# Deformable convolution: nine tap shifts of a pair shared 5 to 4 between SyncE and GpSimd, instead of 4 to 5, late in the second layer

## The reference

```python
off1 = make_offset(conv3x3(x, tm1_w, tm1_b), conv3x3(x, tr1_w, tr1_b))
out = deform_conv(x, off1, dcn1_w)
out = relu(batchnorm(out, bn1_g, bn1_b))
off2 = make_offset(conv3x3(out, tm2_w, tm2_b), conv3x3(out, tr2_w, tr2_b))
out = batchnorm(deform_conv(out, off2, dcn2_w), bn2_g, bn2_b)
return relu(out + residual)
```

## Time and profile before

| what | value |
|---|---|
| median of three runs | 427.45 us (426.53 to 428.62) |
| the profiled execution | 429.34 us, of which the span of the trace is 427.5 us |
| TensorE busy | 398.2 us, 93% of the span |
| ScalarE busy | 327.0 us, 76% |
| VectorE busy | 312.3 us, 73% |
| GpSimd busy | 111.4 us, 26% |
| mean granted clock of TensorE | 0.991 |
| `moved<-conv_sb` DMAs | 112 from SyncE, 140 from GpSimd |
| second layer | from about 220 us to 415 us of the span |

### The profile page before, as it was taken

How to read it: one execution, slowest core, us unless ns; L and a number is a source line. 1 busy time by engine, 2 the same in 40 slices (tenths; PEclk the granted TensorE clock), 3 DMA queues, 4 the chain that set the end, 5 groups by cost and what they waited for, 6 DMA issues and landing times.

```text
span 427.5 us, 19117 instructions
## 1 busy us (share of the span) xinstructions
PE 398.2 (93%) x7747; PEld 357.9 (84%) x7747; DVE 312.3 (73%) x868; ACT 327.0 (76%) x423; POOL 111.4 (26%) x241
## 2 busy tenths in 40 slices
PE   4978899999999999999998899999999998999980
PEld 4865689999999999999885788999999997998870
DVE  3649877788887777777438888877777776777445
ACT  2617788888888898888835878888888887888745
POOL 6303223222222222238001322232222222220000
PEclk9999999999999999999999999999999999999996
DMA  6301342211122222222001231222222222222005
GB/s 220 84 2 34 71 69 48 45 36 36 38 46 46 44 44 46 49 48 41 2 3 28 57 62 38 50 45 46 45 45 45 48 48 47 48 48 40 3 2 196
DMA packets 61529, 21.28 MB, mean 50 GB/s; under 512 B 53798, under 2 KB 61308, under 8 KB 61484
## 3 DMA queue, kind: packets, MB, share of 16 engines
q1 hardware_dynamic: 56588, 18.20, 20.3%
q0 software_dynamic: 4896, 2.43, 2.2%
HBM read 3.23 MB, written 2.10 MB: 12 GB/s over the span
## 4 chain that ended last, share of the span: by engine, by line
PE 85%; DVE 5%; DMA 4%; ACT 2%; issue 2%; SPq 1%; POOL 1%; DVEq 0%; ACTq 0%; POOLq 0%
PE acc_ps L746 54%; PE z_ps L719 12%; PE build_ps L704 8%; PE side_ps L652 3%; PE acc_ps L770 3%; PE side_ps L641 2%; DMA xs<-in_x 2%; PE build_ps L588 1%; DMA moved<-conv_sb 1%; PE acc_ps L598 1%; DMA feat_rows<-feats 1%; ACT raw L563 1%; PE acc_ps L630 1%; SPq L278 1%; ACT S L482 0%
## 5 line engine op out<-in xcount | busy, mean ns | idle before, releaser
L746 PE MATMUL acc_ps<-S,Z 64*64 64x256 f32 x4416 | 279.4, 377 | 1.6 <-issue 0.9
L746 PEld LDWEIGHTS acc_ps<-S,Z 64*64 64x64 f32 x4416 | 225.3, 133 | 19.8 <-issue 3.5
L482 ACT ACTIVATE S<-build_ps,minus 128x1024 f32<-128x1024 f32 x190 | 201.5, 1112 | 30.6 <-PE build_ps L704 30.2
L719 PE MATMUL z_ps<-wz,xflat 64*64 64x192 f32 x1536 | 106.9, 328 | 0.0
L704 PE MATMUL build_ps<-feat_rows,cst 64*64 64x512 f16 x576 | 82.9, 377 | 3.3 <-ACT S L482 1.6
L475 ACT ACTIVATE Z<-z_ps 128x768 f32<-128x768 f32 x96 | 78.2, 814 | 4.9 <-PE z_ps L719 4.9
L719 PEld LDWEIGHTS z_ps<-wz,xflat 64*64 64x64 f32 x1536 | 75.8, 132 | 6.5 <-issue 1.3
L1007 DVE TENSOR_SCALAR S<-build_ps 128x512 f32<-128x512 f32 x96 | 66.1, 688 | 19.1 <-PE build_ps L704 17.3
L278 POOL DMA_DIRECT2D moved<-conv_sb x140 | 71.0, 514 | 20.6 <-POOL conv_sb L371 15.5
L1009 DVE TENSOR_SCALAR S<-build_ps 128x512 f32<-128x512 f32 x96 | 65.3, 680 | 0.0
L371 POOL TENSOR_TENSOR conv_sb<-conv_sb,cst 128x32 f32<-128x32 f32 x28 | 7.5, 269 | 200.5 <-ACT conv_sb L469 200.5
(11 more groups left out here) (116 smaller groups left out, 307.4 us busy)
## 6 DMA issues: line engine op xcount, KB each, us to landing
xs<-in_x SPq DMA_DIRECT2D x4, 512.0 KB, 7.5
out<-raw SPq DMA_DIRECT2D x7, 256.0 KB, 2.5
moved<-conv_sb POOLq DMA_DIRECT2D x56, 11.2 KB
moved<-conv_sb SPq DMA_DIRECT2D x56, 11.2 KB
moved<-conv_sb POOLq DMA_DIRECT2D x56, 11.3 KB
wz<-in_dcn_w POOLq DMA_DIRECT2D x2, 288.0 KB, 4.7
feat_rows<-feats SPq DMA_TRANSPOSE x32, 3.7
moved<-conv_sb SPq DMA_DIRECT2D x28, 12.0 KB
```

What stands on the lines that cost most here:

```text
L482: act.activation(S[:, (parity + b) % 2, half, 0:ACT_TAPS, :], build_ps[:, 0:ACT_TAPS, :], ACT.Relu, bias=minus2[:, :], scale=1.0 if half = ...
L719: mm = pe.matmul(z_ps[halves[c], i, h * BLOCK_COLS:(h + 1) * BLOCK_COLS], xflat[parity][halves[i], pixels], wz[halves[i], layer, h, b * BL ...
L746: mm = pe.matmul(acc_ps[halves[i], g, 0:HW], Z[halves[g], slot, i, half, j * C:(j + 1) * C], S[halves[g], slot, half, j, :].rearrange(by_i ...
```

## The change

For the layer with index 1, and from pair 20 on (the third shift of that layer; pairs 18 and 19 come first), SyncE issues the taps 4, 1, 7, 3, 8 and GpSimd 0, 2, 5, 6. Tap 8 moves from the end of GpSimd's list to the end of SyncE's. The values waited for follow from a new helper. Twelve shifts are concerned (pairs 20 to 31).

```diff
+LATE_SP_TAPS, LATE_POOL_TAPS = SP_TAPS + POOL_TAPS[4:], POOL_TAPS[:4]
+EARLY_PAIRS = 4
...
+        def is_late(T, layer):
+
+            return layer == 1 and not (isinstance(T, int) and T - PAIRS < EARLY_PAIRS)
+
+        def shifts(T, layer, taps, late_taps):
+
+            if not is_late(T, layer):
+                return 16 * len(taps) * by_taps(T, layer)
+            early = by_taps(PAIRS * layer + EARLY_PAIRS - 1, layer)
+            return 16 * len(taps) * early + 16 * len(late_taps) * (by_taps(T, layer) - early)
...
-                move_taps(sp, SP_TAPS, shifted_by_sp)
+                move_taps(sp, LATE_SP_TAPS if is_late(T, layer) else SP_TAPS, shifted_by_sp)
...
-                move_taps(pool, POOL_TAPS, shifted_by_pool)
+                move_taps(pool, LATE_POOL_TAPS if is_late(T, layer) else POOL_TAPS, shifted_by_pool)
...
-                wait(pe, shifted_by_sp, 16 * len(SP_TAPS) * by_taps(T, layer))
-                wait(pe, shifted_by_pool, 16 * len(POOL_TAPS) * by_taps(T, layer))
+                wait(pe, shifted_by_sp, shifts(T, layer, SP_TAPS, LATE_SP_TAPS))
+                wait(pe, shifted_by_pool, shifts(T, layer, POOL_TAPS, LATE_POOL_TAPS))
```

More of the change, by code:

```diff
@@ L463, in copy_taps @@
                 if after_shift:
-                    wait(act, shifted_by_sp, 16 * len(SP_TAPS) * by_taps(T - 1, layer))
-                    wait(act, shifted_by_pool, 16 * len(POOL_TAPS) * by_taps(T - 1, layer))
+                    wait(act, shifted_by_sp, shifts(T - 1, layer, SP_TAPS, LATE_SP_TAPS))
+                    wait(act, shifted_by_pool, shifts(T - 1, layer, POOL_TAPS, LATE_POOL_TAPS))
                 else:
```

## The result

The changed kernel takes 425.72 us, the median of 22 runs (424.66 to 428.71), beside 427.48 us (426.22 to 428.88) for the kernel before, run alternately with it. The ratio is 0.9961, with a 95% interval of 0.9948 to 0.9974: 1.7 us faster (1.1 to 2.2). That lies in the range that was predicted (425.4 to 428.7) and on the side that was forecast, but the gain is more than twice the 0.75 us of the forecast. It lies outside the forecast's own band (426.0 to 427.3), in that of the rival "no cost" (425.5 to 426.0).

A forecast was written before the change was run, and what follows sets the result against it. TensorE was taken to bound the kernel, waiting only for `moved`. The stall's -1.90 us and the fifth tap's +1.15 gave -0.75, from 427.45 to 426.7 us; own range 426.0 to 427.3, eight times in ten 425.4 to 428.7.

The forecast's parts named there:

- no cost: Rival: the stall goes and SyncE's fifth tap costs nothing, 425.55 us, at most 0.52 more; chance 0.18.
- The stall: GpSimd's 2.87 us hole after its 128th tap, delaying TensorE's reading of `moved`; taken as gone with 128 taps, -1.90 us.
- a stall that stays: Rival: the stall is bound to something else and remains, leaving only the fifth tap's cost, 428.6 us; chance 0.16.
- The rule of the Trainium skill: GpSimd's DMAs wait for descriptors while VectorE runs a two-port operation; by it the 1.90 us would stay; the sum left it out.
- The fifth tap: SyncE's added tap takes 0.76 of 0.80 us spare before TensorE's load of `moved`; delays in three shifts cost 1.15 us.
- pair 21's: Delay at pair 21: SyncE's issues end 0.34 us short of the ordinary lead, less the 0.04 left; cost 0.30 us.
- Pair 27's: Delay at pair 27: SyncE's issues end 0.37 us short of the ordinary lead; cost 0.33 us.
- that of the last pair: Delay at pair 31, where a 16 KB instruction fetch runs through the DMA engines meanwhile; load at 382.75 instead of 382.23, 0.52 us.
- TensorE has no slack to win it back in: Step in the sum: the 1.15 us of delays at the readings of `moved` are not recovered by TensorE.
- The longer transpose queue: On SyncE the features' transpose starts 0.76 us later behind the fifth tap; claimed to cost nothing, at most 0.76 a pair.
- the register steps of the new waits: TensorE's waited-for values become sums of two products in looped pairs; 0 to 1.0 us, taken as 0.
- The used-up room: Rival at L652: the fifth tap makes each of twelve pairs 0.29 to 0.58 us late, 430.15 up to 433.7 us; chance 0.11.

The follow-up runs named there:

- the first layer: Kernel before with the same twelve taps moved from GpSimd to SyncE in the first layer (pairs 4 to 15), second layer at four and five; ratio 0.9940.
- early pairs at five: Changed kernel with EARLY_PAIRS = 5, so pair 20 keeps five taps on GpSimd, 129 in all; ratio 1.0028 to the kernel before.
- setup: Kernel before with six of GpSimd's nine small setup DMAs issued by SyncE instead; one run, 430.21 us.
- scratch: Kernel before with dynamic_dma_scratch_size 16384 instead of 32768; one run, 428.91 us beside 428.94.
- 126 taps and ten other copies: Kernel before with all nine taps of every shift on GpSimd and ten small extra weight copies at the second layer's start; one run, 474.62 us.
- six-tap kernel: Changed kernel with six taps on SyncE and three on GpSimd from pair 20 on; ratio 1.0073 to the kernel before.
- The drain: Kernel before, four and five taps throughout, with one GpSimd drain at the start of the second layer; ratios 0.9944, 0.9960 and 0.9958.

## Why the prediction came out as it did

*The stall.* Right. It was read off the chain and the differences, sized at 1.90 us, and tied to a count with one event as evidence and 0.16 left for a stall that stays. Six kernels now place it: 128 taps, none (this change, the first layer); 129 to 140 taps, one, after the 128th (early pairs at five, setup, scratch); 126 taps and ten other copies, after the 128th DMA. What the engine does in the stall, and whether DMAs, their packets or their bytes add up to it, stays open. The rule of the Trainium skill that was weighed (SBUF — State Buffer, the section "SBUF: two separate sides", which has the doors) is not needed for it: with 128 taps VectorE does the same work beside them, and there is no stall.

*The fifth tap.* Mechanism right, size wrong. The step that failed is "Spare: 0.80. The fifth tap takes 0.76 and leaves 0.04". The six-tap kernel measures 1.21 to spare, so 0.45 is left. About 0.2 of the 0.41 missing is the landing: the 0.58 from last packet to landing was read where GpSimd had two DMAs in flight, and I used it as if it were the middle, although I called it the latest. The other 0.2 is room in TensorE, which the sum put at nothing (next paragraph). With 0.45 left, delays of 0.34 and 0.37 us fit in. Of the three that were forecast, pair 21's measured 0.09, with 0.13 back in the next pair, where 0.30 was predicted. Pair 27's isn't there: its issues take 3.81 us, as usual, and the slow shift is pair 26's (4.13), in this profile and in another of the same kernel, with about 0.05 us left of it after the next pair. I had taken the delay for one that belongs to the pair. Only that of the last pair stays: predicted 0.52, measured 0.14 (11.38) in this profile, 0.38 in the other (378.67 at the end of a pair from 367.05). That the fetch there is TensorE's own, as the forecast had it, the traces don't single out: the fetches of q8 are missing between 280 and 360 us, and TensorE, VectorE and ScalarE all loop there.

*"TensorE has no slack to win it back in."* Wrong, and the rows of before said so: after the stalled pair came one of 11.08. I even took the 0.16 off the stall, and then denied it to the small delays. After a late reading the next pair is short by up to 0.16 us: 322.07 to 333.15 is 11.08. A window counts TensorE as busy for all of it either way, with 9.71 us of weight loads in the short pair and 10.68 in the ordinary one before it (length, then busy us of PE, PEld, DVE, ACT, POOL; clock, DMA, GB/s):

```profile
322.07:333.15 11.08, 11.08 (x234) 9.71 (x231) 9.01 (x24) 9.51 (x13) 2.69 (x6) 1.00 0.23 47
310.62:321.86 11.24, 11.24 (x237) 10.68 (x232) 8.97 (x24) 9.63 (x14) 2.70 (x6) 1.00 0.21 43
```

A likely reading is that an ordinary weight load starts ahead of its product, while earlier products still run, and that a late one only uses up this lead. The 5.71 instead of 5.89 us of the six-tap kernel fit it; it was not tried by itself.

*The sum.* In the profiles the twelve pairs go from 125.51 to 123.80 us. Eleven ordinary pairs are 123.64, so the stall and small delays of before were 1.87, and the delays of after are 0.16, where 1.15 was predicted. -1.87 + 0.16 = -1.71. The longer transpose queue and the register steps of the new waits cost nothing that the 11.24 us of an ordinary pair show, as said.

*The rivals.* "The fifth tap costs nothing", 425.55 us at a chance of 0.18, is nearest to the 425.72 measured, and the time fell into its band. That the stated range holds it is owed to this rival, which the range took in, and not to the sum. The used-up room is real, but one tap further on: it is what six taps show. The forecast also said that about 0.5% is what a measurement can tell from no change; the interval of the 22 runs, 0.9948 to 0.9974, leaves 1 out at a gain of 0.4%. As for the room used up in every pair, the forecast gave it 0.11 and a price of 4.6 to 8.1 us; with six taps the twelve pairs pay 5.8 (129.63 us from 254.68 to 384.31, less 123.80).

A version ahead of the changed kernel beyond doubt was not found. The drain stands at 0.9944, 0.9960 and 0.9958 of before, the change at 0.9961 and 0.9971. They ran side by side once (0.9960 and 0.9971), and their intervals overlap. The drain takes one line and leaves SyncE's room alone; it was run with four and five taps, and with the fifth on SyncE in four shifts.

## What to carry to other kernels

Count what GpSimd's DMAs add up to over the whole program. A stall that occurs once, late, with nothing beside it, may belong to a total, and then it can be moved into a stretch where the engine idles anyway, here with one drain.

When room before a wait is read from a trace, take both ends of each lag and carry both into the sum; the nearest row is not the middle. And let a bottleneck's short pair after a long one count as slack, also for small delays. Here a transfer moved to another queue cost most where a layer starts and the reader already waits (1.4 us for four shifts), and little in the steady state (0.16 us for twelve).

## What the runs showed that was not expected

GpSimd's 129th DMA after the setup is issued 2.8 to 2.9 us late in four kernels, and 4.58 us late in a fifth, for a tap of 11 to 12 KB as for a copy of 4.0 KB, and with half the scratch memory as well. Each of these DMAs shows 32 packets, so it may as well be the first after 4,096 packets, or after some 1,456 KB. No second long stall follows up to the 262nd. A drain ahead of it, with 70 taps issued, holds GpSimd for 6.68 us and takes the stall away.
